# Mamba layers of a convolution-attention hybrid: delta spread over the partitions by DMA, later silu, and centring, skip and residual done as matmuls

## The reference

```python
def _mamba_block(seq, ...):                      # C = 96, inner width 192, 16 states
    mu = seq.mean(-1, keepdims=True)
    var = ((seq - mu) ** 2).mean(-1, keepdims=True)
    h = (seq - mu) * rsqrt(var + EPS) * ln_g + ln_b
    xs, z = split(h @ in_w, 2)
    xc = silu(causal_conv4(xs) + conv_b)
    dbl = xc @ xproj_w                           # dt (6), B (16), C (16)
    delta = softplus(dt @ dt_w + dt_b)
    dA = exp(delta[..., None] * A)
    dBx = delta[..., None] * Bm[:, :, None, :] * xc[..., None]
    hstates = scan(h = dA * h + dBx)             # along the positions
    y = einsum('blds,bls->bld', hstates, Cm) + Dp * xc
    return (y * silu(z)) @ out_w                 # seq = seq + this
```

## Time and profile before

| | |
|---|---|
| median of 3 timed runs | 9348.97 us (9338.39 to 9350.82) |
| the profiled execution | 9345.01 us, span 9342.9 us |
| busy over the span | PE 78%, DVE 73%, ACT 53%, POOL 58% |
| DMA | 698.09 MB in 367705 packets, mean 75 GB/s |
| mean granted PE clock | 0.857 |

### The profile page before, as it was taken

How to read it: one execution, slowest core, us unless ns; L and a number is a source line. 1 busy time by engine, 2 the same in 40 slices (tenths; PEclk the granted TensorE clock), 3 DMA queues, 4 the chain that set the end, 5 groups by cost and what they waited for, 6 DMA issues and landing times. The chain is left out here.

```text
span 9342.9 us, 107667 instructions
## 1 busy us (share of the span) xinstructions
PE 7302.2 (78%) x19376; PEld 2489.5 (27%) x19376; DVE 6834.6 (73%) x7955; ACT 4997.8 (53%) x10430; POOL 5443.5 (58%) x4360
## 2 busy tenths in 40 slices
PE   7777777767777777288888888788888886888877
PEld 2222222222222222022222222222222221445433
DVE  6877878858878788558888899388888895532445
ACT  5555555545555555345566666455666664321456
POOL 5666666656666666147777778377777784000325
PEclk8888888878888888689999999889999998996688
DMA  2222222212222222423333343233333343165322
GB/s 52 48 47 47 47 47 47 46 42 49 51 49 51 48 48 45 118 70 79 83 85 85 85 92 86 59 81 82 89 89 89 91 95 82 78 210 162 100 55 76
DMA packets 367705, 698.09 MB, mean 75 GB/s; under 512 B 41415, under 2 KB 109372, under 8 KB 362364
## 3 DMA queue, kind: packets, MB, share of 16 engines
q1 hardware_dynamic: 367420, 695.26, 30.7%
HBM read 568.49 MB, written 126.63 MB: 74 GB/s over the span
## 5 line engine op out<-in xcount | busy, mean ns | idle before, releaser
L591 POOL TENSOR_TENSOR mamba_prod<-mamba_hs,mamba_BC_rep 128x512 f32<-128x512 f32 x1536 | 1935.1, 1267 | 1123.5 <-DVE mamba_hs L533 1113.6
L533 DVE TENSOR_TENSOR_SCAN mamba_hs<-mamba_dA,mamba_carry,mamba_dbx 128x512 f32<-128x512 f32 x1152 | 1464.4, 1271 | 130.1 <-ACT mamba_dA L462 123.4
L462 ACT ACTIVATE mamba_dA<-mamba_delta_rep,mamba_a_neg 128x512 f32<-128x512 f32 x1536 | 1036.9, 679 | 846.7 <-PE mamba_delta_rep L293 795.7
L1539 POOL TENSOR_TENSOR scan_a_prod<-scan_a_hs,scan_a_BC_rep 128x512 f32<-128x512 f32 x768 | 979.2, 1275 | 479.5 <-DVE scan_a_hs L1465 381.6
L1539 POOL TENSOR_TENSOR scan_b_prod<-scan_b_hs,scan_b_BC_rep 128x512 f32<-128x512 f32 x768 | 979.3, 1275 | 469.0 <-DVE scan_b_hs L1465 373.4
L293 PE MATMUL mamba_delta_rep<-mamba_du,mamba_sel 96*128 96x512 f32 x768 | 529.8, 778 | 653.4 <-ACT mamba_dA L462 653.3
L507 DVE TENSOR_TENSOR mamba_dbx<-mamba_u_rep,mamba_BC_rep 128x512 f32<-128x512 f32 x1152 | 790.2, 686 | 111.5 <-PE mamba_u_rep L293 56.9
L1846 POOL TENSOR_TENSOR ffn_sq<-ffn_xm 96x512 f32<-96x512 f32 x64 | 66.2, 1035 | 1156.5 <-DVE ffn_xm L1814 1145.7
L293 PE MATMUL mamba_u_rep<-mamba_du,mamba_sel 96*128 96x512 f32 x768 | 494.3, 731 | 234.8 <-DVE mamba_hs L533 155.4
L256 PE MATMUL mamba_pre<-mamba_h,mamba_w_conv 96*96 96x512 f32 x1024 | 611.0, 719 | 18.7 <-POOL mamba_tails L561 13.4
L1311 ACT ACTIVATE scan_a_dA<-scan_a_delta_rep,scan_a_a_neg 128x512 f32<-128x512 f32 x768 | 518.4, 678 | 156.7 <-PE scan_a_delta_rep L1098 143.5
(11 more groups left out here) (365 smaller groups left out, 14212.3 us busy)
## 6 DMA issues: line engine op xcount, KB each, us to landing
mamba_BC_rep<-bc_units SPq DMA_DIRECT2D x256, 512.0 KB, 9.4
scan_a_BC_rep<-bc_rows SPq DMA_DIRECT2D x512, 256.0 KB, 5.0
scan_b_BC_rep<-bc_rows SPq DMA_DIRECT2D x512, 256.0 KB, 4.8
by_n<-fin_res SPq DMA_DIRECT2D x32, 768.0 KB, 3.3
fmid_src<-by_n SPq DMA_DIRECT2D x32, 768.0 KB, 6.2
by_k<-fmid_res SPq DMA_DIRECT2D x32, 768.0 KB, 4.3
fout_src<-by_k SPq DMA_DIRECT2D x32, 768.0 KB, 4.7
seq<-mamba_xo SPq DMA_DIRECT2D x64, 192.0 KB, 2.1
```

The costliest lines, as they stand in the source:

```text
L462: nc.scalar.activation(dA[:, s % RING_A], delta_rep[:], ACT.Exp, scale=a_neg[:, s:s + 1]).then_inc(s_dA, 1)
L533: nc.vector.tensor_tensor_scan(hs[:, s % RING_H], dA[:, s % RING_A], dbx_bank(s)[:], carry[:, bass.ds(at, 1)], op0=ALU.mult, op1=ALU.add). ...
L591: pool.tensor_tensor(prod[:, (G * u + s) % RING_P], hs[:, s % RING_H], BC_rep[:, u, QUADS + s % QUADS], ALU.mult).then_inc(s_prod, 1)
L1539: pool.tensor_tensor(prod[:, (G * k + s) % RING_P], hs[:, (G * k + s) % RING_H], BC_rep[:, k, 2 + s % 2], ALU.mult).then_inc(s_prod, 1)
```

## The change

- **Delta** goes the way of B and C. POOL writes it to a buffer `delta` of its own; SP, per half, stores it to DRAM, waits for the landing and reads it back in four DMAs into `delta_rep`, now in SBUF with 6 blocks for each of two units. The six selections per unit on PE go. The PSUM bank that this frees takes the output projection (`out_ps`).
- **Centring** is one matmul with `ident - mean_w` in place of mean and subtraction; ACT copies the result to `xm` and squares it, both from PSUM.
- **The skip** is a matmul with `diag(Dp)` that opens the accumulation of `y`; **the residual** is a matmul with `ident` that opens that of `out_ps`. ACT evicts `y` (two halves) and `out_ps`.
- **Steps**: silu 6 to 10, projections 8, 9 to 10, 11, softplus 10 to 14 to 15 to 17, `copy_bc` 12 to 17, `rsqrt` 8 to 11, POOL's `normalise` 9 to 8, `tail` 13 to 11, the additions 14, 15 to 13, 14, `u` 17 to 16.
- **Rings**: exponentials 4 to 6, states 6 to 8. Some buffers are shared in place (`sp_ln`, `rstd`, `ysk`).

```diff
+            def spread_delta(v, half, done, landed):
+                sp.wait_ge(s_delta[half], done)
+                sp.dma_start(delta_rows[v, half], delta[:, half]).then_inc(s_delta_out[half], 16)
+                sp.wait_ge(s_delta_out[half], landed)
+                by_block = delta_rows[v, half].rearrange("(b c) t -> c b t", c=32)
+                for k in range(NB):
+                    sp.dma_start(delta_rep[32 * k:32 * k + 32, v, HB * half:HB * half + HB], by_block
+                                 ).then_inc(s_rep_d[half], 16)
...
                 if has_next:
+                    spread_delta(1 - u, 0, done, landed)
+                    spread_delta(1 - u, 1, done, landed)
                     spread_bc(1 - u, done, landed)
...
-                nc.tensor.matmul(pre[0][0:C], mean_w[:], xin[:, v], start=True, stop=True).then_inc(s_mean, 1)
+                nc.tensor.matmul(pre[0][0:C], centre_w[:], xin[:, v], start=True, stop=True).then_inc(s_mean, 1)
...
+            def project_out(n, u, kh):
+                if kh == 0:
+                    wait(pe, s_xo, n)
+                    pe.wait_ge(s_xres[u], ...)
+                    nc.tensor.matmul(out_ps[:], ident[:], xres[:, u], start=True, stop=False)
                 pe.wait_ge(s_yg, 2 * n + kh + 1)
-                mm = nc.tensor.matmul(pre[1][0:C], w_out[:, kh], yg[:, kh], start=(kh == 0), stop=(kh == 1))
+                mm = nc.tensor.matmul(out_ps[:], w_out[:, kh], ysk[:, kh], start=False, stop=(kh == 1))
...
                 if i == 0:
                     wait(pe, s_ysk, 2 * n + half)
+                    nc.tensor.matmul(y[:], skip_w[:, half], xc[:, u, half], start=True, stop=False)
...
-                        rep_delta(u if b + 1 < BLOCKS else 1 - u, (b + 1) % BLOCKS)
...
             def square(m):
+                nc.scalar.activation(xm[:], pre[0][0:C], ACT.Copy).then_inc(s_xm, 1)
+                nc.scalar.activation(sq[:], pre[0][0:C], ACT.Square).then_inc(s_sq, 1)
+            def evict_y(n, half):
+                act.wait_ge(s_red, 2 * QUADS * n + QUADS * (half + 1))
+                wait(act, s_out, n)
+                nc.scalar.activation(ysk[:, half], y[:], ACT.Copy).then_inc(s_ysk, 1)
+            def evict_out(n):
+                act.wait_ge(s_out, n + 1)
+                wait(act, s_store, 16 * n)
+                nc.scalar.activation(xo[:], out_ps[:], ACT.Copy).then_inc(s_xo, 1)
...
-                    act.wait_ge(s_rep_d, BLOCKS * n + s // QUADS + 1)
-                    wait(act, s_scan, G * n + s - 3)
-                    nc.scalar.activation(dA[:, s % RING_A], delta_rep[:], ACT.Exp, scale=a_neg[:, s:s + 1]
+                    if s in (0, HG):
+                        act.wait_ge(s_rep_d[s // HG], 64 * n + 64)
+                    wait(act, s_scan, G * n + s - RING_A + 1)
+                    nc.scalar.activation(dA[:, s % RING_A], delta_rep[:, u, s // QUADS], ACT.Exp, scale=a_neg[:, s:s + 1]
...
+                    if s == 8 and not (isinstance(n, int) and n == 0):
+                        evict_y(n - 1, 1)
+                    if s == 19:
+                        evict_y(n, 0)
+                    if s == 14 and not (isinstance(n, int) and n == 0):
+                        evict_out(n - 1)
...
-            def centre(m, v):
-            def add_skip(n, u, half):
-            def residual(n, u):
...
             def add_softplus(m, v, half):
                 pool.wait_ge(s_sp, 2 * m + half + 1)
-                wait(pool, s_rep_u, BLOCKS * (m - 1))
-                pool.tensor_tensor(du[:, v, 0, half], sp_relu[:, half], sp_ln[:, half], ALU.add).then_inc(s_du, 1)
+                wait(pool, s_delta_out[half], 16 * m)
+                pool.tensor_tensor(delta[:, half], sp_relu[:, half], sp_ln[:, half], ALU.add).then_inc(s_delta[half], 1)
...
-                    if s == 3 and not (isinstance(n, int) and n == 0):
+                    if s == 5 and not (isinstance(n, int) and n == 0):
                         gate(n - 1, 1 - u, 1)
-                    if s == 16:
+                    if s == 18:
                         gate(n, u, 0)
```

More of the change, by code:

```diff
@@ L207, in body @@
                                  ).then_inc(s_xin[1 - u], 16)
-                wait(sp, s_xo, last)
+                wait(sp, s_out, last)
                 sp.dma_start(xres[:, u], x_in[:, bass.ds(now, 1)].rearrange("c a t -> c (a t)")
@@ L268, in project @@
                 pe.wait_ge(s_silu, m + 1)
-                if half == 0:
-                    wait(pe, s_xo, m - 1)
-                elif has_ahead:
+                if half and has_ahead:
                     pe.wait_ge(s_ln, m + 2)
@@ L343, in body @@
                         next_step(s, n + 1, 1 - u, has_ahead)
-                    if s in (4, 6) and not (isinstance(n, int) and n == 0):
-                        project_out(n - 1, (s - 4) // 2)
+                    if s in (7, 8) and not (isinstance(n, int) and n == 0):
+                        project_out(n - 1, 1 - u, s - 7)
                     at = s - LAG - QUADS * (HB - 1)
@@ L378, in _ @@
             act.wait_ge(s_a, 1)
+            for half in range(2):
+                nc.scalar.activation(skip_w[:, half], ident[:], ACT.Copy, scale=skip[:, half:half + 1]).then_inc(s_diag, 1)
             def rsqrt(m):
                 act.wait_ge(s_var, m + 1)
-                nc.scalar.activation(lnv[:], pre[0][0:C], ACT.Ln, bias=eps[:]).then_inc(s_ln, 1)
+                wait(act, s_xh, m)
+                nc.scalar.activation(rstd[:], pre[0][0:C], ACT.Ln, bias=eps[:]).then_inc(s_ln, 1)
                 act.wait_ge(s_ln, m + 1)
-                wait(act, s_xh, m)
-                nc.scalar.activation(rstd[:], lnv[:], ACT.Exp, scale=-0.5).then_inc(s_rstd, 1)
+                nc.scalar.activation(rstd[:], rstd[:], ACT.Exp, scale=-0.5).then_inc(s_rstd, 1)
             def affine(m):
@@ L507, in times_b @@
                 nc.vector.tensor_tensor(dbx_bank(g)[:], u_rep[b % 2][:], BC_rep[:, v, i], ALU.mult).then_inc(s_dbx, 1)
-            def add_skip(n, u, half):
-                dve.wait_ge(s_red, 2 * QUADS * n + QUADS * (half + 1))
-                wait(dve, s_yg, 2 * n + half - 1)
-                nc.vector.scalar_tensor_tensor(ysk[:, half], xc[:, u, half], skip[:, half:half + 1], y[:],
-                                               op0=ALU.mult, op1=ALU.add).then_inc(s_ysk, 1)
-            def residual(n, u):
-                dve.wait_ge(s_out, n + 1)
-                dve.wait_ge(s_xres[u], 16 * (n // 2 + 1) if isinstance(n, int) else 8 * (n - u) + 16)
-                wait(dve, s_store, 16 * n)
-                nc.vector.tensor_tensor(xo[:], pre[1][0:C], xres[:, u], ALU.add).then_inc(s_xo, 1)
             def body(n, u, has_next, has_ahead):
-                first = isinstance(n, int) and n == 0
                 for s in range(G):
@@ L535, in body @@
                                                  ).then_inc(s_scan, 1)
-                    if s == 3 and not first:
-                        add_skip(n - 1, 1 - u, 1)
-                    if s == 15:
-                        add_skip(n, u, 0)
-                    if s == 7 and not first:
-                        residual(n - 1, 1 - u)
-                    if s == 2 and has_ahead:
-                        centre(n + 2, u)
-            centre(0, 0)
-            centre(1, 1)
             times_b(0, 0, 0)
             bodies(dve, body)
-            add_skip(UNITS - 1, 1, 1)
-            residual(UNITS - 1, 1)
         @block.gpsimd
```

147 lines of the change are left out of this document (70 added, 77 removed).

## The result

| | before | after |
|---|---|---|
| timed runs, median | 9349.9 us (4 runs) | 9470.99 us (9460.35 to 9474.39, 4 runs) |
| ratio | | 1.0129, 95% interval 1.0112 to 1.0147 |
| profiled execution | 9345.0 us | 9472.9 us, span 9471.0 |
| one period, layer 1 | 57.3 us | 59.04 us |

The change makes the kernel 1.3% slower; 9500 us was forecast. Most kernels here had an execution 90 to 160 us shorter than the rest; the profiled one of experiment 8 is of these, and in it the output stage of the Fourier mixer, which no run changes, takes 188 us instead of 298. The page of the kernel after: busy time by engine, DMA, and two of its costliest groups (count, busy us and mean ns, idle before and what ended it).

A forecast was written before the change was run, and what follows sets the result against it. SP's serial DMA chain bounds each unit: 28.8 to delta ready, 28.0 chain, 2.5 to the next scan, period 59.3 against 57.3. 9345 + 124 + 26 = 9495, with evictions 9500 us; range 9180 to 9690, main case 9400 to 9620.

The forecast's parts named there:

- Delta half 0 ready: Compute ahead of SP's first delta store: ready 28.8 us after the unit's first scan, bounds 27.5 and 31.
- The chain: SP's DMA queue, from delta half 0 ready to B and C landed: 28.0 us per unit, bounds 23.5 and 30.
- One sign: SP's queue: the store of delta's second half was to land 5 to 7 us after its issue.
- The lower bound of the chain: Low end of the DMA chain's time per unit: 23.5 us, with terms of 4.0 and 12.6.
- From the landing to the next first scan: VectorE after B and C land: a product, the last scan and another product, 2.5 us.
- Ahead of unit 0: Start of each Mamba layer: the whole chain is bare, first scan at 78.2 instead of 65.03, 13 us per layer.
- The last units: Last unit of each layer, which prepares no successor: to stay at about 44.6 us.
- The cover: VectorE's gains per unit (2.8 work, 7.0 and 3.1 waits) all fall inside its new wait of some 16 us.
- Rival (a): SP's queue: stores not held by reads, only bytes count; periods 56.4 and 50.3, middle 53.4, 9130 us; chance 0.17.
- Rival (b): SP's queue: delta's spreads are cheap, 4.0 us each; period 56.3, 9310 us; chance 0.10.
- Rival (c): Compute is late as well, PE's clock at 0.50 after VectorE's wait; 3.2 us more, period 62.5, 9693 us; chance 0.08.
- Rival (d): The queue is no bound and VectorE runs at 44.6 us per unit; 8580 us; chance 0.05.

The follow-up runs named there:

- experiment 8: From the kernel of experiment 2: projection half with B and C made first, B and C copied a step earlier, softplus of half 1 before half 0; 8686.2 us, ratio 0.928.
- experiment 2: From the changed kernel: B and C ahead of both delta halves in SP's queue, copied by ACT one step earlier; 8905.4 us, ratio 0.950.
- experiment 11: From the kernel of experiment 8: both delta stores issued from ScalarE's own DMA queue, behind the reads of B and C; 8700.1 us.
- experiment 7: From the kernel of experiment 2: stores of B and C and of delta half 0 both issued ahead of all reads; 8795.2 us.

## Why the prediction was right

- **Delta half 0 ready, 28.8**: 28.3 in the mean, 27.7 and 28.8 in alternate units. The count of instructions along ACT and POOL held within half a microsecond.
- **The chain, 28.0**: 27.5. By its terms: store 2.2 (2.1), reads of a half 5.5 (5.5 and 5.4), second store 0.7 behind them (0.4), store of B and C 0.3 (0.2), reads of B and C 13.6 (13.8). B and C land at 55.8 against 56.8. One sign missed: the second store was to land 5 to 7 us after its issue and took 4.1 in the mean. The sum's own terms gave about 4.5, since the four reads ahead of it take 1.7 us to issue. The lower bound of the chain was a slip too: with the terms named it is 24.0, not 23.5.
- **From the landing to the next first scan, 2.5**: this term was mis-sized; 3.3. In the units in which the loop does not turn it is 2.4 to 2.6. In nearly every second unit, where the loop turns, DVE stands again between the last scan and the next product:

```profile
1021.23 0.70 DVE L528 TENSOR_TENSOR mamba_dbx<-mamba_u_rep,mamba_BC_rep 128x512 f32<-128x512 f32 x1 [1.82 <-issue]
```

  That is the row of 20.6 us, 12 times, in the waits above, 1.7 us each: in 24 of the 62 units, so 0.7 of the missing 0.8 in the mean. In each of these 24 turns a packet of instructions starts just ahead of it, and the product follows 2.0 to 2.2 us after that packet's start. Before, the product follows as late (2.0 to 2.6), but the packet starts 1.6 us ahead of the last scan's end and not 0.4. So the long wait ahead seems to lay the fetch bare; no run tests it. The period came out as 59.1 against 59.3 because the errors of 1.0 and 0.8 nearly cancel: the mechanism was right, the closeness in part luck.
- **Ahead of unit 0, 13 us a layer**: 10.3 (75.34 against 65.03) in layer 1 and 8.7 in layer 2; here the sum was 7 us too high for both layers. In layer 1 delta was ready at 48.1 (48.9 forecast) and its chain took 26.0 us instead of 28.0. The last units took 1.9 us less each (42.7 against 44.6), which I had at nothing.
- Sum: 31 x 1.73 = 54 in layer 1, 61 in layer 2, 19 ahead of them, 4 back at their ends: 130, of which the rest of the program took back 2: 128 between the spans. The forecast had 124 + 26 + 5 = 155.
- **The cover**: of 12.9 us of gains per unit, DVE's waits of 7.0 and 3.1 did go, and none of it reached the period. That a DVE without the chain comes to about 44 us also held: scans 0 to 23 run from 0.0 to 43.3 in experiment 8.
- **Rival (a)**, stores not held by reads: refuted (4.4 us in after, 11.3 in experiment 2). The rule of the Trainium skill, DMA: Bandwidth & Descriptors, Queues, rings and completion order, is that a DMA's semaphore increment lands only after every earlier write from that DMA engine (one of the 16 that move the data, not SP or ScalarE), across its queues. The landings on SP's queue fit it, 0.2 to 0.4 us behind the last read; but the 9.1 us of experiment 11 are not shown to come from it, since there the store's first packet starts 6.1 us after the issue.
- **Rival (b)**, spreads of 4.0: refuted behind a landing (5.5), though 3.0 is what one costs behind other reads (experiment 7). **Rival (c)**, late compute: the granted clock fell from 0.82 to 0.79, delta came no later. **Rival (d)** is what experiment 8 approaches once B and C land 16 us earlier.

## What to carry to other kernels

What a round trip through DRAM costs depends on its place in the DMA order: with the same bytes the kernel took 9471 or 8686 us. Put the transfer that the busiest engine needs first at the head, and issue a store before the reads that would hold it, since here a second queue did not free it. Work taken off an engine is worth what the wait behind it does not give back; the offload lay hidden in this kernel, and gave 28 us of the Mamba stretch alone and 113 with the chain shortened. Here moving B and C ahead of delta, and the projection that makes them ahead of the other, turned a loss of 1.3% into a gain of 7.2%.

## What the runs showed of the hardware

- A 192 KB store on ScalarE's queue, issued behind 2 MB of reads on SP's, lands after 9.1 us instead of 2.1, and its first packet starts after 6.1 (experiment 11).
- Four reads of 192 KB take 5.6 us from an empty queue and add 3.0 us behind other reads (experiments 2 and 7).
- The total of bytes, 824 MB against 698, is not what sets the time here: experiment 8 moves the same bytes as after, in 785 us less, and is faster than before. In the chain bytes still count: 3.0 us for each 768 KB even behind other reads.
